# The last phase of an attention and expert layer: root scratch in PSUM, a ring of three bank pairs, sums moved between engines

## The reference

```python
yk = out[slot].reshape(T, K, H)
y = jnp.sum(yk * topk_w[..., None].astype(yk.dtype), axis=1)
shared = jax.nn.silu(x @ Sg.T) * (x @ Su.T) @ Sd.T
return (y + shared).reshape(B, S, H)
...
x = x + _layernorm(...)     # (v - mean) / sqrt(var + 1e-5) over the 256 columns
```

## Time and profile before

| | us |
|---|---|
| Median of 3 runs | 1404.93 (1403.07 to 1407.63) |
| The profiled execution, its own time | 1400.53 |
| Its span in the profile | 1398.8 |
| TensorE busy in the span | 1232.7 (88%) |
| Pool busy | 925.7 (66%) |
| VectorE busy | 875.7 (63%) |
| ScalarE busy | 832.7 (60%) |
| First load of the last phase issued | 1337.57 |
| Last instruction starts | 1391.77 |

### The profile page before, as it was taken

How to read it: one execution, slowest core, us unless ns; L and a number is a source line. 1 busy time by engine, 2 the same in 40 slices (tenths; PEclk the granted TensorE clock), 3 DMA queues, 4 the chain that set the end, 5 groups by cost and what they waited for, 6 DMA issues and landing times.

```text
span 1398.8 us, 25701 instructions
## 1 busy us (share of the span) xinstructions
PE 1232.7 (88%) x7872; PEld 857.2 (61%) x7872; DVE 875.7 (63%) x2413; ACT 832.7 (60%) x2256; POOL 925.7 (66%) x1112
## 2 busy tenths in 40 slices
PE   3589999899999989989989998999966999999984
PEld 1356556576666666656666665666633677778953
DVE  5677657678668767867876876786666322222237
ACT  2476558677777777767677776777744332323413
POOL 3577646468886976878788697788855513444554
PEclk9899999999999999999999999999987999999977
DMA  6467697645655454444435444454434559898683
GB/s 201 101 164 166 168 240 151 167 82 119 128 108 103 85 106 94 83 95 80 93 72 91 91 78 80 82 80 85 80 87 139 162 151 238 224 233 215 133 247 121
DMA packets 364489, 182.70 MB, mean 131 GB/s; under 512 B 287248, under 2 KB 343030, under 8 KB 364352
## 3 DMA queue, kind: packets, MB, share of 16 engines
q1 hardware_dynamic: 344768, 166.18, 51.4%
q0 software_dynamic: 16416, 11.70, 4.7%
q10 hardware_dynamic: 3168, 3.15, 0.7%
HBM read 75.32 MB, written 64.69 MB: 100 GB/s over the span
## 4 chain that ended last, share of the span: by engine, by line
PE 34%; DVE 16%; POOL 16%; DMA 13%; ACT 11%; issue 10%; SPq 0%; ACTq 0%; POOLq 0%; DVEq 0%
DMA Y<-W,wix 7%; PE bank L927 6%; POOL PH L864 5%; POOL P L859 5%; DMA PT<-PH 5%; PE bank L956 5%; ACT P L1186 4%; PE bank L971 4%; POOL BUF L626 4%; PE bank L1033 3%; PE bank L942 3%; PE bank L1090 3%; PE bank L988 2%; PE bank L1049 2%; PE bank L1103 2%
## 5 line engine op out<-in xcount | busy, mean ns | idle before, releaser
L864 POOL TENSOR_TENSOR PH<-P,PH 128x512 f16<-128x512 f32 x256 | 300.3, 1173 | 169.8 <-ACT PH L1195 167.1
L927 PE MATMUL bank<-RB,W 128*128 128x512 f16 x1092 | 282.0, 384 | 17.1 <-DVE RB L377 14.0
L956 PE MATMUL bank<-RB 128*128 128x256 f32 x1024 | 252.2, 388 | 33.7 <-DVE RB L1299 13.1
L859 POOL TENSOR_SCALAR P<-P,rr 128x256 f32<-128x256 f32 x512 | 247.7, 492 | 47.3 <-DVE rr L1320 47.3
L1186 ACT ACTIVATE P<-bank,nm 128x256 f32<-128x256 f32 x512 | 237.9, 475 | 26.2 <-DVE nm L1324 19.1
L626 POOL DMA_INDIRECT BUF<-RT,ix x192 | 201.7, 1051 | 67.9 <-issue 35.7
L971 PE MATMUL bank<-PT,RB 128*128 128x256 f16 x1536 | 213.9, 276 | 33.7 <-DVE O L1330 24.6
L956 PEld LDWEIGHTS bank<-RB 128*128 128x128 f32 x1024 | 184.6, 191 | 70.8 <-issue 22.9
L1195 ACT ACTIVATE PH<-P 128x512 f16<-128x512 f32 x256 | 163.4, 638 | 91.1 <-POOL P L859 52.6
L971 PEld LDWEIGHTS bank<-PT,RB 128*128 128x128 f16 x1536 | 147.2, 99 | 107.8 <-issue 46.1
L1178 ACT ACTIVATE O<-bank,bqk 128x256 f16<-128x256 f32 x256 | 123.2, 481 | 125.0 <-PE bank L971 124.9
(11 more groups left out here) (200 smaller groups left out, 1675.0 us busy)
## 6 DMA issues: line engine op xcount, KB each, us to landing
RB<-in_ewT SPq DMA_DIRECT2D x24, 352.0 KB
BUF<-zrow SPq DMA_DIRECT2D x4, 1926.0 KB, 8.8
W<-BUF SPq DMA_DIRECT2D x64, 120.4 KB, 4.1
HT<-in_ewT SPq DMA_DIRECT2D x18, 352.0 KB
HT<-in_wc SPq DMA_DIRECT2D x24, 256.0 KB, 3.6
HT<-in_ws SPq DMA_DIRECT2D x24, 256.0 KB, 4.1
Y<-zrow SPq DMA_DIRECT2D x10, 512.0 KB, 3.1
RB<-in_ewd SPq DMA_DIRECT2D x24, 176.0 KB
```

Source lines behind the costliest of these rows:

```text
L859: r = eng.tensor_scalar(p, p, rr[:, w % 4, t:t + 1], SP_, ALU.mult, ALU.mult)
L864: eng.tensor_tensor(PH[:, w % 2, 1, :], P[:, w % 2, :], PH[:, w % 2, 0, :], ALU.subtract).then_inc(s["pl"], 1)
L927: r = eng.matmul(bk_[:, :], W[:, m, a, c * 2048 + h * 128:c * 2048 + (h + 1) * 128], XT[:, bp % 2, b, c, :], start=(k == 0), stop=(k == n ...
L956: r = eng.matmul(bS[u % 2][:, t * 256:(t + 1) * 256], QK[:, i % 2, 0, q * 256 + t * 128:q * 256 + (t + 1) * 128], QK[:, i % 2, 1, q * 256: ...
```

## The change

Five edits, all in the last phase:

- The last pair of banks, `(bP0, bP1)`, leaves `LB_`; the groups turn over three pairs (`NL` = 3). Three columns of 32 in `bP0` (`root`) become the scratch of the root steps.
- The root steps are written anew. The variance plus epsilon, the intermediate and the last iterate are in PSUM, the estimate `y` is in SBUF, so that no step has two inputs in SBUF. `v*y*y` is formed in another order. A copy of the result to SBUF is added, since ScalarE reads its scale there; the bias is formed from the PSUM copy.
- For groups 0 and 1 (`PE_SUM` = 2) Pool's sum is left out; TensorE adds both loaded arrays by matmuls with the identity and waits for the load itself.
- For groups 0 to 5 (`DVE_X1` = 6) Pool adds both halves of the residual; VectorE keeps the second half of groups 6 and 7. SyncE's wait for VectorE falls away for the first six.
- Pool's order is written anew.

```diff
-POOL_LAST = "s0 s1 s2 s3 x0 s4 x1 s5 x2 x3 s6 s7 x4 x5 x6 x7"
+POOL_LAST = "s2 s3 s4 x0 x1 s5 s6 x2 s7 x3 x4 x5 x6 x7"
+PE_SUM = 2
+DVE_X1 = 6
...
-        LB_ = ((bACC[0], bACC[1]), (bV, bO), (bS[0], bS[1]), (bP0, bP1))
+        LB_ = ((bACC[0], bACC[1]), (bV, bO), (bS[0], bS[1]))
+        NL = len(LB_)
+        root = bP0[:, 0:96].rearrange("p (k t) -> p k t", k=3)
...
-                eng.wait_ge(s["fy"], g + 1)
+                if g >= DVE_X1:
+                    eng.wait_ge(s["fy"], g - DVE_X1 + 1)
...
             def last_x1(g):
                 f = fin[g]
-                eng.wait_ge(s["fn"], 2 * g + 1)
...
-                eng.tensor_tensor(half(f[:, 0], 0), half(f[:, 0], 0), half(x1[g], 0), ALU.add).then_inc(s["fx"], 1)
+                for h in range(2 if g < DVE_X1 else 1):
+                    eng.wait_ge(s["fn"], 2 * g + h + 1)
+                    r = eng.tensor_tensor(half(f[:, 0], h), half(f[:, 0], h), half(x1[g], h), ALU.add)
+                r.then_inc(s["fx"], 1)
...
             def last_over(g):
-                if g >= 4:
-                    eng.wait_ge(s["fn"], 2 * (g - 4) + 2)
+                if g >= NL:
+                    eng.wait_ge(s["fn"], 2 * (g - NL) + 2)
...
             def last_add(g):
-                eng.wait_ge(s["fa"], g + 1)
+                if g < PE_SUM:
+                    eng.wait_ge(s_fl[g], 32)
+                else:
+                    eng.wait_ge(s["fa"], g - PE_SUM + 1)
+                parts = (0, 1) if g < PE_SUM else (0,)
                 for t in range(4):
-                    r = eng.matmul(LB_[g % 4][t // 2][:, t % 2 * 256:(t % 2 + 1) * 256], ident[:, :],
-                                   fin[g][:, 0, t, :], start=False, stop=(t % 2 == 1), skip_group_check=True)
+                    for k in parts:
+                        r = eng.matmul(LB_[g % NL][t // 2][:, t % 2 * 256:(t % 2 + 1) * 256], ident[:, :],
+                                       fin[g][:, k, t, :], start=False, stop=(t % 2 == 1 and k == parts[-1]),
+                                       skip_group_check=True)
                 r.then_inc(s["fp"], 1)
 
-            for g in range(4):
+            for g in range(NL):
                 last_over(g)
             for g in range(NP):
-                if g >= 4:
+                if g >= NL:
                     last_over(g)
                 last_add(g)
...
-                v, y, a, b = (fNW[:, k, c0:c1] for k in range(4))
+                v, b, yp = (root[:, k, c0:c1] for k in range(3))
+                y, bias = fNW[:, 1, c0:c1], fNW[:, 3, c0:c1]
                 step(eng.tensor_scalar(v, fMV[:, c0:c1, 1], EPS, None, ALU.add))
                 step(eng.tensor_scalar(y.bitcast(I32), v.bitcast(I32), -0.5, RSQRT_MAGIC, ALU.mult, ALU.add))
                 for k in range(3):
-                    step(eng.tensor_tensor(a, y, y, ALU.mult))
-                    step(eng.scalar_tensor_tensor(out=b, in0=a, scalar=-0.5, in1=v, op0=ALU.mult, op1=ALU.mult))
-                    step(eng.scalar_tensor_tensor(out=y, in0=b, scalar=1.5, in1=y, op0=ALU.add, op1=ALU.mult))
-                eng.scalar_tensor_tensor(out=b, in0=fMV[:, c0:c1, 0], scalar=-1.0, in1=y, op0=ALU.mult, op1=ALU.mult
+                    step(eng.tensor_tensor(b, v, y, ALU.mult))
+                    step(eng.scalar_tensor_tensor(out=b, in0=b, scalar=-0.5, in1=y, op0=ALU.mult, op1=ALU.mult))
+                    step(eng.scalar_tensor_tensor(out=y if k < 2 else yp, in0=b, scalar=1.5, in1=y,
+                                                  op0=ALU.add, op1=ALU.mult))
+                eng.tensor_copy(y, yp)
+                eng.scalar_tensor_tensor(out=bias, in0=fMV[:, c0:c1, 0], scalar=-1.0, in1=yp, op0=ALU.mult, op1=ALU.mult
                                          ).then_inc(s["fs"], 1)
...
-                if n:
-                    for g in BATCH[n - 1]:
+                for g in BATCH[n - 1] if n else ():
+                    if g >= DVE_X1:
                         last_x1(g)
```

More of the change, by code:

```diff
@@ L1121, in last_over @@
             def last_over(g):
-                if g >= 4:
-                    eng.wait_ge(s["fn"], 2 * (g - 4) + 2)
+                if g >= NL:
+                    eng.wait_ge(s["fn"], 2 * (g - NL) + 2)
                 for t in range(4):
-                    eng.matmul(LB_[g % 4][t // 2][:, t % 2 * 256:(t % 2 + 1) * 256],
+                    eng.matmul(LB_[g % NL][t // 2][:, t % 2 * 256:(t % 2 + 1) * 256],
                                W95T[:, (4 * g + t) * 128:(4 * g + t + 1) * 128], OUT95[0:E, :],
@@ L1129, in last_over @@
                     for t in range(4):
-                        eng.matmul(LB_[g % 4][t // 2][:, t % 2 * 256:(t % 2 + 1) * 256], ident[:, :],
+                        eng.matmul(LB_[g % NL][t // 2][:, t % 2 * 256:(t % 2 + 1) * 256], ident[:, :],
                                    YL[g][:, t, :], start=False, stop=False, skip_group_check=True)
             def last_add(g):
-                eng.wait_ge(s["fa"], g + 1)
+                if g < PE_SUM:
[3 more added lines that the diff above has]
+                parts = (0, 1) if g < PE_SUM else (0,)
                 for t in range(4):
-                    r = eng.matmul(LB_[g % 4][t // 2][:, t % 2 * 256:(t % 2 + 1) * 256], ident[:, :],
-                                   fin[g][:, 0, t, :], start=False, stop=(t % 2 == 1), skip_group_check=True)
+                    for k in parts:
+                        r = eng.matmul(LB_[g % NL][t // 2][:, t % 2 * 256:(t % 2 + 1) * 256], ident[:, :],
+                                       fin[g][:, k, t, :], start=False, stop=(t % 2 == 1 and k == parts[-1]),
+                                       skip_group_check=True)
                 r.then_inc(s["fp"], 1)
-            for g in range(4):
+            for g in range(NL):
                 last_over(g)
             for g in range(NP):
-                if g >= 4:
+                if g >= NL:
                     last_over(g)
@@ L1281, in _ @@
                         c = 4 * g + t
-                        r = eng.activation(fin[g][:, 0, t, :], LB_[g % 4][h][:, t % 2 * 256:(t % 2 + 1) * 256],
+                        r = eng.activation(fin[g][:, 0, t, :], LB_[g % NL][h][:, t % 2 * 256:(t % 2 + 1) * 256],
                                            ACT.Identity, bias=fNW[:, 3, c:c + 1], scale=fNW[:, 1, c:c + 1])
@@ L1400, in last_stats @@
                     for t in range(4):
-                        r = eng.bn_stats(fST[g][:, t, :], LB_[g % 4][t // 2][:, t % 2 * 256:(t % 2 + 1) * 256])
+                        r = eng.bn_stats(fST[g][:, t, :], LB_[g % NL][t // 2][:, t % 2 * 256:(t % 2 + 1) * 256])
                 step(r)
@@ L1419, in last_x1 @@
                 eng.wait_ge(s["fn"], 2 * g + 2)
-                if g < 4:
-                    eng.wait_ge(s["xr"], 64)
                 eng.tensor_tensor(half(f[:, 0], 1), half(f[:, 0], 1), half(x1[g], 1), ALU.add).then_inc(s["fy"], 1)
```

## The result

The changed kernel takes 1410.56 us, median of 15 runs (1405.98 to 1417.66), against 1404.47 (1401.66 to 1407.63) for the kernel before. That is +6.1 us, slower by more than the 0.3% bound. The ratio of the two sets of runs on record is 1.0051, 95% interval 1.0036 to 1.0067; the medians by themselves give 1.0043. The forecast was 1412.7, +7.8, slower.

A forecast was written before the change was run, and what follows sets the result against it. In the last 65 us TensorE, then VectorE, bound the kernel; with three bank pairs, VectorE's freed time becomes waiting for TensorE. Ring +3.3 and clock +4.5 make +7.8 on 1404.93: 1412.7 us, range 1405 to 1421.

The forecast's parts named there:

- Stalls that go: VectorE's root steps beside Pool: 8.7 us of stalls vanish and 3.6 us of additions leave, freeing 12.3 us.
- What the PSUM scratch costs: Root steps with PSUM scratch: 0.20 us a step, one more step per batch; bounds -1.2 and +4.0 us in all.
- Extra work at the start: TensorE before group 1's statistics: eight more instructions cost 1.92 us; ScalarE's batch 0 starts 2.1 us later.
- The ring of three: Group 3's overflow matmuls wait for ScalarE to drain group 0; loop 10.7 us, end moves +3.3 us at full clock.
- The clock in the ring: TensorE idles 4.9 and 3.1 us, then runs at half clock: two slowed pieces, then one, 1.5 us each, +4.5 us.
- Pool: Pool's 26 additions, 32.5 us, fit the 46 us left; sums ready five and ten us early; costed at nothing.
- Ports still shared: Rival: small root steps still wait for Pool despite the PSUM operand, in batches 1 and 2; 1416.2 us, chance 0.06.
- Ring, clock full: Rival: TensorE's clock dips don't come or fall on pieces with slack; +3.3 us, 1408.2 us, chance 0.20.
- VectorE's chain stays the bound: Rival: VectorE's freed 12.3 us come out at the end, less added costs; -9.4 us, 1395.5 us, chance 0.07.

The follow-up runs named there:

- scratch_sbuf: Changed kernel with only the root steps' scratch in SBUF, three pairs; stretch (first overflow matmul to end of VectorE's last addition) 69.5 us, ratio 1.0095.
- keep_busy_ring: Changed kernel plus nine and five matmuls, results unread, into unused bP1 in TensorE's two idle gaps behind groups 2 and 4; stretch 61.8 us, ratio 1.0019.
- ring3_alone: Kernel before with three bank pairs instead of four, nothing else of the change; stretch 67.7 us, ratio 1.0040.
- x1_moved_alone: Kernel before with only the residual's additions for groups 0 to 5 moved to Pool, in changed order; stretch 63.2 us, ratio 1.0024.
- four_pairs_sbuf: Changed kernel with four bank pairs again and the root steps' scratch in SBUF; stretch 67.2 us, ratio 1.0048.
- ring7_keep_start: Changed kernel with a ring of seven single banks, half a group each, plus fifteen unread matmuls at the start; stretch 55.3 us, ratio 1.0048.
- ring6_keep_all: Changed kernel with a ring of six single banks, half a group each, plus unread matmuls at the start and in ring gaps; stretch 56.4 us, ratio 1.0065.

## Why the prediction was right

Its sign, its number and its main mechanism held: the ring of three puts TensorE's wait for ScalarE on the path, and the clock falls there. That the sum came so near is in part luck, since sizes that were off cancel. By its own steps, each as the time between two starts of ScalarE's batches:

| part | before | forecast | after |
|---|---|---|---|
| to batch 0 | 23.8 | +2.1 | 24.8 (+1.0) |
| batch 0 to 1 | 9.9 | 10.7 and 3.0 for the clock | 14.2 |
| batch 1 to 2 | 10.7 | 10.7 and 1.5 | 11.8 |
| batch 2 to 3 | 6.4 | 5.3 | 5.25 |
| batch 3 to 4 | 5.3 | 6.9 | 6.8 |
| last pass and addition | 2.9 | 2.9 | 3.0 |

- **Stalls that go**: right, and shown by scratch_sbuf: 3.7 us of stretch come back with the scratch in SBUF. The rows of the kernel before have 9.0 us of stalls, 8.7 was taken; none of the changed kernel's steps stalls. They are 65, thirteen in each of five batches; the prediction's bounds count 62, which changes them by no more than 0.2 us.
- **What the PSUM scratch costs**: 0.20 us a step was taken, 0.205 measured, 2.53 us for thirteen steps of batch 0 against 2.6. The estimate by the Trainium skill's figure (VectorE: DVE Perf Modes, errata section), 65 ns more a step, is not borne out for these small instructions: 5 ns.
- **Extra work at the start**: 1.92 us forecast, 0.9 measured (group 1's statistics 20.1 us after the first matmul instead of 19.2). The sum took the half level to end as long behind the first matmul as before; in this execution it ended 2 to 3 us sooner. So about 1 us of the term is put down to luck of the clock; with four pairs, where TensorE has 16 instructions more ahead of group 1's statistics instead of 8, they come 4.4 us later.
- **The ring of three**: right in place and size. TensorE's idle time ahead of group 3 was 4.96 us for 4.9 forecast; the second turn of keep_busy_ring, at full clock, is 10.6 us for 10.7; ring3_alone shows the wait without the other edits.
- **The clock in the ring**: right that it falls and that it is now on the path; the sizes were off in two ways that cancel. A slow piece costs 1.8 us, not 1.5, and four in a row were slow and a fifth in part (2.44 us), where the forecast had two in the first turn and one in the second. On the other hand the second gap never came: TensorE was still on group 4 when ScalarE released group 5, so of the later slow pieces only the rest, about 1.1 us, reached the path. Forecast 4.5 us; the turns give 3.5 and 1.1, 4.6. The rule of the Trainium skill (TensorE: Matmul & The Clock Gate, HAM oscillation), that waits between bursts make the next burst start cold, agrees with these rows in that the slow stretch begins behind the 4.96 us.
- **Pool** at nothing: right in the changed kernel. The sums of groups 5 and 7 were ready 11 us before TensorE wanted them, where the prediction had five and ten. But it holds only with the scratch in PSUM and the ring as cover: by itself the move costs 4.1 us (x1_moved_alone), by stalls.
- **Rivals**: "Ports still shared" is out, as no step stalls beside Pool. "Ring, clock full" is out for this execution, by 16 us at 0.50. "VectorE's chain stays the bound" is out, by VectorE's 8.21 us of idle time for TensorE. I had given it as what the change would be without the ring, 9.4 us faster. `four_pairs_sbuf` is not a test of that, as it has its roots in SBUF; ring7_keep_start at full clock comes nearest, 3.8 us of stretch below before, and not 9.4.

What the prediction did not see is that the costs don't add. The ring alone is +8.6 us, 6.6 of them in its two turns, but on top of the other edits in SBUF (four_pairs_sbuf to scratch_sbuf) only +2.3, 3.6 in the two turns less 1.5 at the start, since time in which VectorE waits for TensorE covers time in which it would wait for Pool. So "the ring costs x" has no single value here. Four pairs with the scratch in PSUM were not run: the four pairs are all eight banks, and the scratch needs one.

Open is what decides between the two clusters of ring7_keep_start and ring6_keep_all: the runs at the higher time have the lower mean clock, but no trace is of one of them, so where in the span the clock was lost is not shown.

## What to carry to other kernels

A bank taken from a ring of accumulators for scratch is paid for where the ring turns: work out the loop from one release to the next (drain, refill, statistics, roots) and compare it with the time that the consumer needs. If the loop is longer, the fast consumer only waits. And when the wait sits on TensorE, price its pieces at half clock too, since the gap that the wait makes can bring the clock down just where the work has come onto the path.

An engine's freed time is no gain when the work goes to an engine whose instructions block small ones elsewhere. Here moving 3.6 us of additions to Pool brought VectorE 7.6 us of stalls while the small steps had all their operands in SBUF, and none once each had an input or its output in PSUM.

## What the runs showed of the hardware

- A root step with its inputs and output in SBUF waits for the end of a running Pool addition (1.14 to 1.25 us), a two-input one and a one-input `tensor_scalar` alike; with one side in PSUM it takes 0.17 us beside Pool. A step of 128x8 that writes PSUM takes 0.17 us, as does one that writes SBUF.
- The half level lasts much longer than the gap ahead of it: 16 us behind a gap of 4.96 us with TensorE busy for 14.8 of 16, and 26 us behind one of 3.19 us with TensorE busy for 25.85 of 26. In the kernel before it was over after 3 to 4 us (0.50 from 1362 to 1364, 0.67 to 1366), with gaps of 2.64 and 0.88 us ahead of it.
- A short gap can stand ahead of the half level too: in keep_busy_ring TensorE was idle for 0.89 us up to 1351.17, with work without a break before it, and the clock was at 0.77 in the stretch from 1352 and at 0.50 in that from 1354.
- The time of one program can fall into two clusters that differ in the granted clock: ring7_keep_start has three runs at 1391 to 1394 us (0.970 to 0.973) and nine at 1403 to 1409 (0.957 to 0.969), with nothing between. That the clock is the cause is not shown.
